# Reordering VectorE's work at the head of each graph in a fused hypergraph-convolution and expert-layer kernel

## The reference, cut to what matters

```
xn  = layernorm(x)
A1  = Be * (H^T xn)            # first aggregation over nodes, Be = 1/column count
h   = layernorm(relu(Dn * (H A1) W1 + b1))
y   = Dn * H (Be * H^T (h W2)) + b2 + xn
x1  = x + y
x2  = layernorm(x1)
mask = softmax weights of the two largest of 4 router logits (x2 @ router_w + router_b)
comb = sum_e mask_e * silu(x2 @ expert_w[e] + expert_b[e])
out = x1 + norm_w * rmsnorm(x2 + comb @ out_w + out_b)
```

## Time and profile before

| | |
|---|---|
| median of 3 runs | 835.37 us (833.93 to 835.69) |
| the profiled execution | 831.88 us |
| its span, first to last instruction | 830.3 us |
| TensorE busy | 743.3 us (90%) |
| VectorE busy | 696.3 us (84%) |
| ScalarE busy | 507.9 us (61%) |
| GpSimd busy | 327.6 us (39%) |
| mean granted TensorE clock | 0.967 of full |

### The profile page before, as it was taken

One profiled execution on the slowest core, in us unless ns is written; L12 is line 12 of the kernel. 1 busy time (PEld: TensorE's weight loads), 2 busy tenths in 40 slices (PEclk: granted clock), 3 DMA queues, 4 the chain that ended last, 5 costly groups with the idle time before them and its releaser, 6 DMA issues.

```text
span 830.3 us, 16479 instructions
## 1 busy us (share of the span) xinstructions
PE 743.3 (90%) x5584; PEld 488.6 (59%) x5584; DVE 696.3 (84%) x1551; ACT 507.9 (61%) x1024; POOL 327.6 (39%) x606
## 2 busy tenths in 40 slices
PE   3556999999999999999999999999999999999872
PEld 2245475675848476574848576574848566574631
DVE  3655889989898989989898989989898989989752
ACT  4345666757675665757675666767575666756441
POOL 4123516344361616345260626345261625443222
PEclk9869799999999999999999999999999999999985
DMA  8101204040221304041230404031220404011022
GB/s 244 57 0 29 100 2 102 27 102 27 77 51 30 75 22 101 25 97 29 76 51 7 94 25 101 25 90 36 76 51 0 101 25 101 0 29 24 26 26 25
DMA packets 37416, 45.32 MB, mean 55 GB/s; under 512 B 2832, under 2 KB 28560, under 8 KB 37392
## 3 DMA queue, kind: packets, MB, share of 16 engines
q1 hardware_dynamic: 28688, 36.62, 13.5%
q0 software_dynamic: 8704, 8.39, 8.6%
HBM read 28.23 MB, written 16.78 MB: 54 GB/s over the span
## 4 chain that ended last, share of the span: by engine, by line
PE 52%; DVE 28%; issue 10%; ACT 6%; POOL 3%; DMA 0%; POOLq 0%; DVEq 0%; ACTq 0%
PE bank L1025 11%; PE bank L1026 10%; PE bank L1027 10%; PE bank L1103 6%; PE bank L1102 6%; DVE yf L847 4%; PE bank L1070 3%; DVE lsel L821 3%; DVE a1l L788 3%; PE bank L1063 3%; DVE z L753 2%; DVE xtl L912 2%; DVE xbn L634 2%; ACT xsh L403 2%; PE bank L1078 1%
## 5 line engine op out<-in xcount | busy, mean ns | idle before, releaser
L445 ACT ACTIVATE silu<-bank,ebcol,ksc 128x512 f32<-128x512 f32 x128 | 98.6, 770 | 56.5 <-PE bank L1027 56.1
L374 POOL TENSOR_TENSOR yme<-yms,epsrms 128x4 f32<-128x4 f32 (+1 forms) x17 | 3.4, 201 | 298.6 <-ACT ysq L480 298.6
L1025 PE MATMUL bank<-xth,ewh 128*128 128x512 f16 x256 | 98.9, 386 | 0.8 <-DVE ewl L667 0.8
L1026 PE MATMUL bank<-xtl,ewh 128*128 128x512 f16 x256 | 98.4, 384 | 0.0
L1027 PE MATMUL bank<-xth,ewl 128*128 128x512 f16 x256 | 98.0, 383 | 0.0
L1025 PE MATMUL bank<-w2h,hnth 128*128 128x256 f16 x256 | 70.5, 275 | 0.0
L1026 PE MATMUL bank<-w2l,hnth 128*128 128x256 f16 x256 | 70.4, 275 | 0.0
L1027 PE MATMUL bank<-w2h,hntl 128*128 128x256 f16 x256 | 70.4, 275 | 0.0
L1122 PE MATMUL bank<-ht,a1h 128*128 128x512 f16 x128 | 50.8, 397 | 12.7 <-DVE a1l L788 12.7
L1155 PE MATMUL bank<-xsh,h 128*128 128x256 f16 x256 | 58.4, 278 | 4.1 <-DVE xsl L647 2.2
L745 DVE TENSOR_TENSOR silu<-silu,bank 128x1024 f32<-128x1024 f32 x48 | 58.4, 1216 | 3.9 <-ACT silu L445 2.5
(11 more groups left out here) (193 smaller groups left out, 2202.9 us busy)
## 6 DMA issues: line engine op xcount, KB each, us to landing
adjin<-adj SPq DMA_DIRECT2D x16, 1024.0 KB, 5.3
xin<-x SPq DMA_DIRECT2D x16, 512.0 KB, 3.5
out<-x SPq DMA_DIRECT2D x16, 512.0 KB, 4.1
out<-yf POOLq DMA_DIRECT2D x32, 256.0 KB, 4.5
ewf<-ew SPq DMA_DIRECT2D x1, 1024.0 KB, 9.4
w1f<-w1t SPq DMA_DIRECT2D x1, 512.0 KB, 7.7
w2f<-w2t SPq DMA_DIRECT2D x1, 512.0 KB, 7.9
b1b<-b SPq DMA_DIRECT2D x1, 256.0 KB, 8.1
```

The lines of the kernel that those rows point to most:

```text
L445: af(silu[:, i % 4, :], bank[E_BANK[i]][:, :], ACT.Silu, bias=ebcol[:, i:i + 1], scale=ksc[:, 2:3]).then_inc(silu_dn, 1)
L1025: mm(outp, lh, rh, start=first, stop=False)
L1026: mm(outp, lh, rl, start=False, stop=False)
```

## The change

Only VectorE's written order at the head of a body changes. No instruction is added or removed, and no tile, semaphore or wait is new.

```diff
                 if conv and ffn and not late:
                     setup_lo(c_hi, 2, ((rwf, rwh, rwl, RW), (owf, owh, owl, OW)), c_lo)
+                if conv:
+                    a1_part(g, 0)
+                    a1_part(g, 1)
                 if late:
                     finish(q, (0, 1), not ffn, not (isinstance(g, int) and g == 2))
-                if conv:
-                    a1_part(g, 0)
-                if late:
-                    finish(q, (2, 3), not ffn, False)
-                if conv:
-                    a1_part(g, 1)
                 if conv and not ffn:
                     setup_lo(a_hi, 1, ((w1f, w1h, w1l, W1),), a_lo)
-                if prep and ffn:
-                    prep_x_stats(g + 1)
                 if ffn:
                     for j in range(2):
                         dve.wait_ge(xt_hi, 2 * f + j + 1)
                         s = slice(256 * j, 256 * j + 256)
                         STT(xtl[:, :, s], bank[XT_BANK[j]][:, :].rearrange("p (k c) -> p k c", k=KD), XS,
                             xth[:, :, s], ALU.mult, ALU.subtract).then_inc(xt_lo, 1)
+                if late:
+                    finish(q, (2, 3), not ffn, False)
                 if conv and ffn and not late:
                     setup_lo(c_hi, 3, ((ewf, ewh, ewl, EX),), c_lo)
+                if prep and ffn:
+                    prep_x_stats(g + 1)
                 if conv:
                     d_vector(g)
```

## The result

The changed kernel takes 845.14 us (median of 4 runs, 843.66 to 847.3) against 835.39 us of the kernel before (4 runs, 833.93 to 835.69). The medians are 9.8 us apart; the ratio is 1.0112, interval 1.009 to 1.0134. The forecast was 843.4 us, 8.0 us slower, in a range of 837.0 to 847.5.

The account below looks back on a forecast made before the run. The prediction took the statistics of the next x (dsum, xmv, x2o, lsel, mask, mt) to bound a graph. Bodies 2 to 14 add 7.2 us, the others 0.8: 8.0 us slower, from 835.37 to 843.4, range 837.0 to 847.5.

Parts of the forecast that it names:

- Steps 1 to 4: Steady graph's head, a1l pairs to xtl: TensorE's gaps of 0.59 and 0.60 go; first yf pair's hold shrinks to 0.20.
- Step 5: Second yf pair, 0.80 us; GpSimd's second store, 1.20, costs nothing, covered by GpSimd's wait of 2.84.
- Step 6: Statistics behind xtl on VectorE, 1.31 us: dsum starts at 419.73 instead of 419.18, 0.55 us later.
- Step 7: From xmv to mt all comes 0.55 later; new TensorE waits of 1.0 and some 0.6; period grows 0.55 us.
- What `xb` holds: Which VectorE instructions GpSimd's xb holds: yf, with two SBUF inputs, not a1l; if a1l too, 10.5 us instead of 7.2.
- The other bodies: Bodies outside 2 to 14: body 1 0.6, body 15 -0.5, body 16 +0.7; together +0.8 us.
- The four terms: Bodies 2 to 14 7.2 us, body 1 0.6, body 15 -0.5, body 16 +0.7; sum 8.0 us slower.
- the ends: Bodies 1, 15 and 16: between 0 and 1.3, -0.84 and +0.5, 0 and +2; taken together as +0.8 us.
- the steady term: Bodies 2 to 14: each 0.55 us longer, 13 x 0.55 = 7.2 us.
- Faster: Rival, second half of a2 and router: TensorE's waits go, nothing replaces them; 15.3 us less 0.8, 820.9 us; 9%.
- Absorbed: Rival, wait for mt: later statistics are absorbed, 836.2 to 837.8 us; 6% for the half that counts as no change.
- The hold belongs to `yf`: Rival, first yf pair: takes 2.66 us wherever it stands, period grows 1.1 more, 14.6 us on top, 858; 4%.

Follow-up runs that it names:

- two_more_stats: Kernel before with two more bn_stats of x per body (bodies 2 to 14) between xtl and dsum; 845.06 us, ratio 1.0097.
- the two x2o moves: GpSimd's x2o moved behind the scales of h: on the kernel before 828.48 us, ratio 0.9924; on the changed kernel 827.33 us, ratio 0.9896.
- stats_back: Changed kernel with the four statistics of the next x put back ahead of xtl, behind the first yf pair; 838.18 us, ratio 1.003.
- fill: Kernel before reordered: first yf pair, first a1l pair, statistics, second a1l pair, second yf pair, xtl; 817.02 us, ratio 0.9754.
- new_end: Kernel before in bodies 1 to 14, the changed order in bodies 15 and 16 only; 839.91 us, ratio 1.005.
- after_again: Changed kernel as it is, measured again in a second series against the kernel before; 847.11 us, ratio 1.0127.
- after_x2o_late: Changed kernel with GpSimd's x2o moved behind the scales of h of the same body; 827.33 us, ratio 0.9896.

## Why the prediction was right, point by point

- **What sets the time of a graph: right.** The chain was said to go through dsum, xmv, x2o, lsel, mask and mt, and not through TensorE's waits for `a1l` and `xtl`. `two_more_stats` lengthened it without touching those waits (8.5 us for an expected 8.6), the period followed the end of `x2o` within 0.01 us in six kernels, and the two x2o moves cut the chain at `lsel` and gave 7 us and 18 to 20 us.
- **Steps 1 to 4: right, small errors.** The forecast idle times 0.70, 0.96 and 0.54 were 0.74, 0.87 and 0.54; the first `yf` pair took 0.93 us, less than the 1.1 forecast. `xb` ends at 419.96, and the second `yf` of the pair at 420.65. GpSimd's times were not kept as they were: `xb` ends 0.16 us earlier after `h` than before.
- **Step 5: right at its place, with less cover than its words say.** The store hides, but the cover fell to 0.86 us. The step had left out 0.66 us between the end of a `yf` pair and the issue of its store (415.96 to 416.62 in the earlier trace rows); with it the store ends 14.27 us after `h`, as measured, where the step had 13.7. `stats_back` shows what it costs when the cover is gone: `x2o` ends 0.3 us later than in the kernel before.
- **Step 6: 0.55 was 0.49.** `xth` came 0.07 us earlier in the body than I had it. Over bodies 2 to 14 it makes 6.5 us instead of 7.2.
- **Step 7: right.** The new waits of 1.0 and 0.6 are 1.21 and 0.64, that for `mt` is still 0.43, and the period is 47.52 (47.6 forecast). The wait for `a2l` is larger than forecast by what TensorE gained more ahead of it.
- **What `xb` holds: right for the instructions that it meets here.** In `fill` the statistics run inside `xb` and take their 1.40 us, and the second `a1l` pair, but for its last 0.13 us inside it too, takes 0.86. But two SBUF inputs are not what every held instruction has: `dclip`, with one, was held for 2.07 us by `x2o` in body 15 of the kernel before.
- **The other bodies: the term that was mis-sized.** "Together +0.8" measured 0.70 + 1.65 in bodies 1 and 15, and up to 1.69 in the last piece. The step that failed is body 15: I took the bound near the gain of 0.84 us, from TensorE's wait, and put the late `x2o` at +0.5. `x2o` lay on the steps of Dn already in the kernel before, ahead of both `a2l`, where TensorE had no slack; the late store makes it end 2.08 us later there, and TensorE waits 2.79 us. The trace of the kernel before had the held `dclip`, so this could have been worked out. The four terms measured 10.5 us where 8.0 were forecast: the ends were 3.2 too low, and the steady term, 0.7 too high, hid part of it. That the median lay in the range owes something to luck: its upper bound, 12.1 us above the kernel before, takes 10.5 for the steady bodies and does not cover the 3.8 that the ends' own upper bounds add up to, and the steady bodies stayed well under their bound.
- **The rivals.** Faster (TensorE's waits go and nothing replaces them): these waits did go, and others replaced them. Absorbed: no, `mt`'s wait kept its length to 0.01. The hold belongs to `yf`: no, the pair took 0.93 at its new place.

## What to carry to other kernels

When instructions of one engine are put in another order, write down when each one's input is ready: an instruction that is pulled ahead of its input does not run earlier, it turns the filler that stood ahead of it into idle time, and the filler is then paid for later on the path. Here the same instructions, placed so that ready work covers each wait, were some 28 us faster than the order that puts the urgent ones first (817 against 845 us, from two series; ratios 0.9754 and 1.0112 to the kernel before). And before a wait of the busiest engine is worked on, follow that engine to its next wait: if another chain ends there, the time gained only moves.

## What the runs showed of the hardware that I had not expected

**A wait near 2.8 us of TensorE can cost more than its length.** In `new_end` the same wait of 2.79 us for `a2l` in body 15 is followed by matmuls of 0.61 and 0.63 us, in the changed kernel by 0.39 and 0.38. Stretches of `new_end` (us, busy time and count of PE, PEld, DVE, ACT, POOL, granted clock, DMA share, GB/s):

```profile
748.00:756.00 8.00, 7.53 (x60) 3.96 (x58) 6.75 (x12) 4.55 (x9) 5.53 (x4) 1.00 0.43 43
756.00:760.00 4.00, 1.69 (x5) 0.58 (x6) 3.72 (x12) 0.00 (x0) 0.77 (x1) 0.77 0.29 45
760.00:764.00 4.00, 4.00 (x17) 1.56 (x16) 2.78 (x8) 2.01 (x4) 0.00 (x0) 0.80 0.00 0
764.00:770.00 6.00, 6.00 (x29) 2.39 (x28) 5.25 (x15) 4.30 (x8) 3.23 (x12) 1.00 0.01 3
```

and of the changed kernel around the same wait:

```profile
759.00:763.00 4.00, 1.52 (x7) 0.70 (x8) 3.76 (x11) 0.00 (x0) 0.94 (x1) 1.00 0.33 50
763.00:767.00 4.00, 4.00 (x22) 1.78 (x21) 3.51 (x10) 2.62 (x5) 0.00 (x0) 1.00 0.00 0
```

The granted clock fell from full to a mean of 0.77 over the stretch with the wait (part of it at the lower level of 1.2 GHz) in one execution and stayed at 2.4 GHz in the other, with the same instructions in that body and the same wait. Body 15 took 50.89 us in `new_end` and 49.29 in the changed kernel, 1.6 us more; of the other traces with that wait, it took 50.98 in `stats_back`, with a granted clock of 0.84 and 0.73 in two stretches of 4 us, and 49.29 in `after_again`. The Trainium skill, TensorE: Matmul & The Clock Gate, Part 1, calls the throttled clock the default, from which activity releases the engine; the trace agrees as far as it goes, since full speed came back only after matmuls had run again. That this is why the nine runs of `new_end` lie at 838.4 to 839.9 and at 841.7 to 842.3 with nothing in between fits, but only one of them has a profile, and the mean granted clock of the whole run (0.963 to 0.965 in the slower four, 0.963 to 0.971 in the others) does not tell them apart.

**The issue of a store by GpSimd did not hold the VectorE instructions that `x2o` and `xb` hold.** In `after_x2o_late` `dn` starts at 742.37, inside the issue of the second store, and takes its 0.16 us. Timeline of GpSimd and then of VectorE of that kernel:

```profile
742.14 1.20 POOL L351 DMA_DIRECT2D out<-yf  x1 [1.42 <-DVE yf L847]
```

```profile
742.37 0.16 DVE L801 SCALAR_TENSOR_TENSOR dn<-dsum,drec 128x4 f32<-128x4 f32 x1
742.57 0.32 DVE L803 TENSOR_SCALAR dna<-dn,ksc 128x4 f32<-128x4 f32 x1
```

In body 8 of the changed kernel the second `yf` pair starts at 422.40, inside the issue of the first store (421.40 to 422.66), and takes its 0.87 us. In body 15 of the changed kernel, with `x2o` right behind the same store, `dn` at that place is held from its start, 0.5 us before the recorded start of `x2o`; GpSimd's spans are rough.

**Which instruction is held can turn on hundredths of a microsecond.** In a short body of `stats_back` `lsel` starts at 332.54, just ahead of `x2o` at 332.56, and takes 0.17 us; `arg`, two instructions later, is held in its place and takes 2.01 us, until `x2o` has ended at 334.93, so that body is only 0.1 us shorter than one of the kernel before. In a long body `lsel` starts at 426.74 and `x2o` at 426.76, the same 0.02 us apart in the record, and `lsel` takes 2.40 us.
